# A GRU that runs one tile behind its attention instead of two, with VectorE's and ScalarE's work per tile dealt out to the chunks anew

## The chip, the cores and the metric

The kernel runs on one core of one Trainium2 chip. Its engines are TensorE (PE in the rows, PEld for its weight loads), VectorE (DVE), ScalarE (ACT), GpSimd (POOL) and SyncE (SP, which only issues DMAs here). Each engine works through its own list of instructions in order and meets the others only through semaphores. The metric is the device time of one execution in microseconds (us).

## The reference

For 4096 tokens of 256 features: a layer norm, a graph attention over a dense 0/1 adjacency matrix of 4096 x 4096, a GRU cell on the attention's result, a second layer norm, and a mixture of 16 experts of which each token uses two.

```
Wh = h @ W                                   # h = layernorm(x)
e = leaky_relu(Wh @ a1 + (Wh @ a2).T, 0.2)
att = softmax(where(adj > 0, e, -9e15))
h_prime = att @ Wh
gi = h_prime @ w_ih.T + b_ih ; gh = h @ w_hh.T + b_hh
r = sigmoid(i_r + h_r) ; z = sigmoid(i_z + h_z) ; n = tanh(i_n + r * h_n)
x = x + (1 - z) * n + z * h                  # called x1 below
x = x + experts(layernorm(x))                # top 2 of 16 by softmax(ln(x) @ gate_w + gate_b)
```

## The kernel before

There are three stages: a preparation of all 32 token tiles (up to about 115 us), the attention stage (about 115 to 843 us), which this change is about, and the routing tables with the 79 expert slots after it.

The attention stage handles one tile of 128 query tokens per round, against all 4096 keys. Keys are taken in chunks of 512, `CPT` = 8 chunks per tile; masks and exponentials are taken in quarters of 1024, `Q` = 4 per tile. Every engine has a hand-written function `body(i)` that is unrolled for i = 0, 1, ...; what an engine does in a round, and in which order, is the order of the lines in its `body`. `live(i, lag)` says whether tile i - lag exists. For tile i:

- ScalarE `logits(i, q)` (L546) and VectorE `less_one(i, q)` (L729, adjacency minus one), `mask_logits(i, q)` (L735), `row_max(i)` (L744, L745), then ScalarE `weights(i, q)` (L551, the exponential). This is made in round i - 1, one tile ahead. `row_max` needs all four masks and `weights` needs `row_max`.
- For each chunk TensorE transposes four 128 x 128 blocks into a PSUM bank (`transpose_weights`, L1012 on `E`), ScalarE copies the bank's high part (`chunk_hi`, L482 into `pc`), VectorE makes the low part (`chunk_lo`, L751), and TensorE adds 12 matmuls to the tile's sum (`accumulate`, L1106 to L1108). Transposes, `chunk_hi` and `chunk_lo` run two chunks ahead of `accumulate`, with three buffers each.
- When a tile's eight chunks are done, VectorE `combine` (L757, L760, divides the sum) and `remake_xn` (L767), TensorE `transpose_h` (L1012 on `scr` and `xnb`), ScalarE `copy_hT` (L482 into `hT`), TensorE `gru` (L1130, L1133, 16 matmuls), VectorE `gru_logits` (L772, L773), ScalarE `rz_tanh` (L573), VectorE `gru_n` (L778, L780), ScalarE `n_tanh` (L577), VectorE `gru_out` (L786 to L791, writes x1).
- Then the second norm: VectorE `norm2` (L796 to L798, then, when GpSimd's power L434 is done, L802 writes `xrow`), TensorE `transpose_x2` (L1012 on `xrow`), ScalarE `copy_x2T` (L482 into `xn2T`), TensorE `gate` (L1154), VectorE `route_top` (L809 to L816), ScalarE `gate_exp` (L587), VectorE `route_weights` (L822 to L824), after which SyncE stores the token's row.

Before, round i works on the sums of tile i, the GRU of tile i - 2 and the gate of tile i - 3, and there are T + 3 = 35 rounds, three of them behind the last sum. After the last round TensorE counts ranks (L1186), which waits for `route_weights` of the last tile and opens the routing stage.

Of the kernel before, what the change touches and what calls it, by code (L numbers as in the profile page):

```python
# [35 lines left out]
def gnn_moe(nc, x, adj, W, a, w_ih, w_hh, b_ih, b_hh, gate_w, gate_b, w1, w2, w3, out, rows):  # L36
# [24 lines left out]
    with ctx:  # L61
# [197 lines left out]

        block = ctx.enter_context(nc.Block())  # L260

        LAST = T + 3

        def live(i, lag):

# [48 lines left out]
        @block.sync  # L314
        def _(sp):
            row = lambda b, lo, hi: b[lo:hi].rearrange("(o f) -> o f", o=1).broadcast_to([P, hi - lo])
            xg4 = x.rearrange("(g r p) f -> g p r f", r=4, p=P)

            def load_x(g):
                k = g % 4  # L320
                if g >= 4:
                    sp.wait_ge(s_xn, (g - 3) * 4)
                sp.dma_start(xs[:, k * 4:k * 4 + 4, :], xg4[g]).then_inc(s_x[k], 16)

            load_x(0)
            sp.dma_start(Wn[:, :, :], W.rearrange("(k p) f -> p k f", p=P)).then_inc(s_cld[0], 16)
            sp.dma_start(a_row[:, :], a.rearrange("f o -> o f").broadcast_to([P, 2 * F])).then_inc(s_cld[1], 16)
            load_x(1)
            sp.dma_start(wnat[:, 0, :, :], w_ih.rearrange("(r p) f -> p r f", p=P)).then_inc(s_wn[0], 16)
            load_x(2)  # L330
            sp.dma_start(wnat[:, 1, :, :], w_hh.rearrange("(r p) f -> p r f", p=P)).then_inc(s_wn[1], 16)
            load_x(3)
            sp.dma_start(gwt[:, :, :], gate_w.rearrange("(k p) e -> p k e", p=P)).then_inc(s_cld[2], 16)
            sp.dma_start(gbias[:, :], row(gate_b, 0, NE)).then_inc(s_cld[3], 16)
            sp.dma_start(bias_rz[:, :], row(b_ih, 0, 2 * F)).then_inc(s_bld, 16)
            sp.dma_start(bhh_rz, row(b_hh, 0, 2 * F)).then_inc(s_bld, 16)
            sp.dma_start(bias_n[:, 0:F], row(b_ih, 2 * F, 3 * F)).then_inc(s_bld, 16)
            sp.dma_start(bias_n[:, F:2 * F], row(b_hh, 2 * F, 3 * F)).then_inc(s_bld, 16)
            for g in range(4, NG):
                load_x(g)  # L340

            def body(i):
                u = i % 2
                if live(i, 1):
                    v = (i - 1) % 2
                    if i >= 3:
                        sp.wait_ge(s_x1, i - 2)
                    sp.dma_start(xin[:, v, :], x[(i - 1) * P:i * P, :]).then_inc(s_xr[v], 16)
                if live(i, 2):
                    sp.wait_ge(s_x1, i - 1)  # L350
                    sp.dma_start(out[(i - 2) * P:(i - 1) * P, :], x1).then_inc(s_x1s, 16)
                if live(i, 3):
                    sp.wait_ge(s_row, i - 2)
                    sp.dma_start(rows[(i - 3) * P:(i - 2) * P, :], xrow[:, (i - 3) % 2, :]).then_inc(s_rows[(i - 3) % 2], 16)

            for i in range(LAST):
                body(i)


            w1v, w2v = (w.rearrange("e (p k) h -> e p (k h)", k=KB) for w in (w1, w2))  # L360
            w3v = w3.rearrange("e (p k) o -> e p (k o)", k=HB)
            sp.wait_ge(s_tab, 3)

            def load(s, r, m, st):

                if st == SLOTS:
                    return
                e, new, b = (table(sp, k, s) for k in (EXPERT, NEW, BUF))
                waits = []
                if st is None or st >= GR:  # L370
                    waits.append((s_whi, s * 2 + (1 - 2 * GR)))
                if st is None or st >= WB:
                    waits.append((s_fy, s - (WB - 1)))
                if waits:
                    wait_apart(sp, *waits)
                for n, wv in enumerate((w1v, w2v, w3v)):
                    sp.dma_start(wexp[:, one(b), n, :].rearrange("p o f -> p (o f)"),
                                 wv[one(e), :, :].rearrange("o p f -> (o p) f"), cond=new == 1).then_inc(s_w[r], 16)

            slot_iterations(sp, load)  # L380
            sp.wait_ge(s_sc, 16 * SLOTS)
# [3 lines left out]
        def _(pool):  # L385
# [39 lines left out]
                load_adj(1, q)  # L425

            def body(i):
                if i + 2 < T:
                    for q in range(Q):
                        pool.wait_ge(s_ms, (i + 1) * Q + q + 1)  # L430
                        load_adj(i + 2, q)
                if live(i, 2):
                    pool.wait_ge(s_var2, i - 1)
                    nc.gpsimd.tensor_tensor(rs[:, :], var[:, :], mhalf[:, :], ALU.pow).then_inc(s_rs2, 1)  # L434

            for i in range(LAST):
                body(i)
# [43 lines left out]
        def _(act):  # L481
# [103 lines left out]
            def gate_exp(i):  # L585
                act.wait_ge(s_dl, i - 2)
                nc.scalar.activation(rt[:, 1:2], rt[:, 0:1], ACT.Exp).then_inc(s_de, 1)  # L587

            def body(i):
                if live(i, 3):  # L590
                    act.wait_ge(s_t2, i - 2)
                    act_copy(xn2T[:, :, :].rearrange("p k m -> p (k m)"), tp[:, 0:F]).then_inc(s_t2e, 1)
                if i + 1 < T:
                    for q in range(Q):
                        logits(i + 1, q)
                for c in range(CPT):
                    if live(i, 0):
                        chunk_hi(i * CPT + c + 2)
                    if 1 <= c < 1 + Q and i + 1 < T:
                        weights(i + 1, c - 1)  # L600
                    if c == 2 and live(i, 2):
                        rz_tanh(i)
                    if c == 5 and live(i, 1):
                        copy_hT(i)
                    if c == 4 and live(i, 2):
                        n_tanh(i)
                    if c == 4 and live(i, 3):
                        gate_exp(i)

            for i in range(LAST):  # L610
                body(i)
# [54 lines left out]
        def _(dve):  # L666
# [123 lines left out]
                    dve.wait_ge(s_x1s, (i - 2) * 16)  # L790
                V_.tensor_tensor(x1, dd, xin[:, u, :], ALU.add).then_inc(s_x1, 1)  # L791

            def norm2(i):
                u = i % 2
                dve.wait_ge(s_x1, i - 1)
                link(V_.bn_stats(bst[:, 0, :], x1))  # L796
                link(V_.bn_aggr(mv[:, :], bst[:, 0, :]))
                V_.tensor_scalar(var[:, :], mv[:, 1:2], EPS, None, ALU.add).then_inc(s_var2, 1)  # L798
                dve.wait_ge(s_rs2, i - 1)
                if i >= 4:  # L800
                    dve.wait_ge(s_rows[u], ((i - 4) // 2) * 16 + 16)
                V_.tensor_scalar(xrow[:, u, 0:F], x1, mv[:, 0:1], rs[:, 0:1], ALU.subtract, ALU.mult).then_inc(s_ln2, 1)  # L802
# [39 lines left out]

            def body(i):
                ahead = i + 1 < T
                if ahead:
                    less_one(i + 1, 0)
                    less_one(i + 1, 1)
                if live(i, 1):
                    combine(i - 1)
                    remake_xn(i - 1)  # L850
                if ahead:
                    mask_logits(i + 1, 0)
                    less_one(i + 1, 2)
                    mask_logits(i + 1, 1)
                    less_one(i + 1, 3)
                    mask_logits(i + 1, 2)
                for c in range(CPT):
                    if live(i, 0):
                        chunk_lo(i * CPT + c + 2)
                    if c == 0 and ahead:  # L860
                        mask_logits(i + 1, 3)
                        row_max(i + 1)
                    if c == 1 and live(i, 2):
                        gru_logits(i)
                    if c == 2 and live(i, 3):
                        route_top(i)
                    if c == 3 and live(i, 2):
                        gru_n(i)
                    if c == 4 and live(i, 3):
                        route_weights(i)  # L870
                    if c == 5 and live(i, 2):
                        gru_out(i)
                    if c == 6 and live(i, 2):
                        norm2(i)

            for i in range(LAST):
                body(i)
# [132 lines left out]
        def _(pe):  # L1010
# [150 lines left out]
            transpose_weights(1)  # L1161

            def body(i):
                if live(i, 3):
                    transpose_x2(i)
                if live(i, 2):
                    gru(i)
                if live(i, 3) and not live(i, 0):
                    gate(i)
                for c in range(CPT):  # L1170
                    if live(i, 0):
                        transpose_weights(i * CPT + c + 2)
                        accumulate(i, c)
                    if c == 0 and live(i, 3) and live(i, 0):
                        gate(i)
                    if c == 3 and live(i, 1):
                        transpose_h(i)

            for i in range(LAST):
                body(i)  # L1180
# [90 lines left out]
```

## Time and profile before

| | |
|---|---|
| median of 3 runs | 1316.3 us (1313.3 to 1320.53) |
| the profiled execution | 1322.15 us, span 1320.4 us |
| busy share of the span: PE, PEld, DVE, ACT, POOL | 91%, 78%, 77%, 59%, 27% |
| TensorE clock, mean over the span | 0.945 of full speed |
| attention stage, 250 to 700 us: busy share PE, DVE, ACT | 98%, 85%, 67% |
| between 830 and 900 us: busy share PE, DVE | 43%, 82% |

The shares are of different stages: TensorE is busy nearly all the time in the attention rounds and in the expert slots, and waits at the end of the attention stage and through the routing tables. The profiled execution's own time beside its span leaves 1.75 us around it.

### The profile page before, as it was taken

The numbers are of one execution on the slowest core, as the hardware profiler recorded it, in microseconds if no ns is written. First come the engines' busy times: TensorE is split into PE (matmuls) and PEld (weight loads), VectorE is DVE, ScalarE is ACT, GpSimd is POOL, SyncE is SP. The second block draws the span as 40 slices with busy tenths as digits, with TensorE's granted clock in tenths as the row PEclk, the third lists the DMA queues.
The fourth block names the chain that finished last, engine by engine and source line by source line (L and its number), as shares of the span: only waits on it lengthen the run. The fifth ranks groups of instructions, "written<-read, shape, count | busy, mean of one in ns | idle before, by whom it ended". The sixth has DMA issues, their size and how long they took to land.

```text
span 1320.4 us, 25406 instructions
## 1 busy us (share of the span) xinstructions
PE 1195.2 (91%) x7317; PEld 1035.0 (78%) x7319; DVE 1019.8 (77%) x2445; ACT 779.5 (59%) x1141; POOL 355.0 (27%) x351
## 2 busy tenths in 40 slices
PE   5675999999999999999999997259999999999995
PEld 4445888888888898989898986148888888888884
DVE  5336788888888888888888875688888888888883
ACT  3227666666666666666666652006666666666662
POOL 1322111010101011111111100015656555555553
PEclk9767999999999999999999998659999999999998
DMA  6204424242424242424243400042354364345430
GB/s 200 56 1 64 63 55 77 57 77 57 77 57 77 57 77 56 77 57 77 57 77 57 77 25 21 13 150 53 52 137 96 55 187 135 91 93 146 93 48 8
DMA packets 61630, 98.60 MB, mean 75 GB/s; under 512 B 9472, under 2 KB 36096, under 8 KB 61536
## 3 DMA queue, kind: packets, MB, share of 16 engines
q0 software_dynamic: 33600, 52.49, 25.3%
q1 hardware_dynamic: 27936, 44.93, 10.5%
q8 instruction: 50, 0.82, 0.3%
q14 instruction: 44, 0.36, 0.1%
HBM read 213.18 MB, written 18.81 MB: 176 GB/s over the span
## 4 chain that ended last, share of the span: by engine, by line
PE 61%; DVE 16%; DMA 9%; ACT 6%; issue 4%; POOL 3%; POOLq 0%; DVEq 0%; SPq 0%; ACTq 0%
PE bank L1221 11%; PE bank L1012 11%; DMA out<-ysc,cidx 9%; PE bank L1130 8%; PE bank L1235 7%; PE bank L1107 5%; PE bank L1106 5%; PE bank L1108 5%; PE bank L1133 4%; DVE pc L751 3%; ACT E L551 2%; PE bank L1040 2%; ACT pc L482 1%; POOL rs L434 1%; DVE scr L788 1%
## 5 line engine op out<-in xcount | busy, mean ns | idle before, releaser
L1106 PE MATMUL bank<-V,pc 128*128 128x258 f32 x1024 | 311.2, 304 | 3.5 <-DVE pc L751 3.5
L1107 PE MATMUL bank<-V,pc 128*128 128x258 f32 x1024 | 291.6, 285 | 0.0
L1108 PE MATMUL bank<-V,pc 128*128 128x258 f32 x1024 | 289.3, 283 | 0.0
L482 ACT ACTIVATE pc<-bank 128x512 fp32r<-128x512 f32 x256 | 152.1, 595 | 173.0 <-PE bank L1012 169.6
L1221 PE MATMUL bank<-wup,xT 128*128 128x512 f32 x948 | 239.4, 401 | 0.9 <-DVE xT L959 0.9
L751 DVE TENSOR_TENSOR pc<-bank,pc 128x512 fp32r<-128x512 f32 x256 | 176.4, 689 | 64.4 <-ACT pc L482 59.9
L1221 PEld LDWEIGHTS bank<-wup,xT 128*128 128x128 f32 x948 | 174.4, 191 | 35.1 <-DVE xT L959 1.3
L1106 PEld LDWEIGHTS bank<-V,pc 128*128 128x128 f32 x1024 | 194.0, 189 | 4.6 <-DVE pc L751 4.6
L1108 PEld LDWEIGHTS bank<-V,pc 128*128 128x128 f32 x1024 | 196.1, 192 | 0.0
L1107 PEld LDWEIGHTS bank<-V,pc 128*128 128x128 f32 x1024 | 196.1, 191 | 0.0
L954 DVE TENSOR_TENSOR wup<-wexp,wup 128x1024 fp32r<-128x1024 f32 x158 | 185.8, 1217 | 2.3 <-ACT wup L482 1.4
L462 POOL DMA_INDIRECT out<-ysc,cidx x79 | 138.6, 1755 | 168.0 <-DMA out<-ysc,cidx 79.6
L482 ACT ACTIVATE wup<-wexp 128x1024 fp32r x158 | 165.6, 1050 | 9.2 <-DMA wexp<-in_L_ffn_w 8.6
L1012 PE MATMUL bank<-ident,E 128*128 128x128 f32 x1024 | 156.6, 276 | 13.4 <-ACT E L551 13.4
L735 DVE CUSTOM_DVE_ANT_0 E<-E,adjb 128x1024 f32<-128x1024 f32 x128 | 158.8, 1241 | 4.1 <-ACT E L546 3.8
L551 ACT ACTIVATE E<-E,nmu 128x1024 f32<-128x1024 f32 x128 | 146.3, 1145 | 11.8 <-DVE nmu L745 11.5
L1235 PE MATMUL bank<-wexp,hidT 128*128 x632 | 149.9, 380 | 1.3 <-ACT hidT L482 0.8
L387 POOL DMA_DIRECT2D adjb<-in_adj x128 | 69.5, 543 | 253.2 <-DVE dmx L735 249.5
L1012 PEld LDWEIGHTS bank<-ident,E 128*128 128x128 f32 x1024 | 122.9, 145 | 17.9 <-issue 14.9
L546 ACT ACTIVATE E<-Dp,sS 128x1024 f32<-128x1024 f32 x128 | 136.2, 1138 | 0.0
L1235 PEld LDWEIGHTS bank<-wexp,hidT 128*128 128x128 f32 x632 | 114.6, 191 | 14.0 <-issue 1.6
L434 POOL TENSOR_TENSOR rs<-var,mhalf 128x1 f32<-128x1 f32 x32 | 18.0, 561 | 391.1 <-DVE var L798 391.1
(155 smaller groups left out, 1645.4 us busy)
## 6 DMA issues: line engine op xcount, KB each, us to landing
wexp<-in_L_ffn_w SPq DMA_DIRECT2D x237, 512.0 KB
adjb<-in_adj POOLq DMA_DIRECT2D x128, 256.0 KB, 4.6
token_rows<-xrow SPq DMA_DIRECT2D x32, 130.0 KB, 2.2
E<-in_x SPq DMA_DIRECT2D x8, 512.0 KB, 5.3
xin<-in_x SPq DMA_DIRECT2D x32, 128.0 KB, 2.7
out<-xin SPq DMA_DIRECT2D x32, 128.0 KB, 1.7
xg<-token_rows,gidx POOLq DMA_INDIRECT x79, 3.6
out<-ysc,cidx POOLq DMA_INDIRECT x79, 3.8
```

The lines of the kernel that those rows point to most:

```text
L462: nc.gpsimd.indirect_dma_start(out=out[:, :], out_offset=bass.IndirectOffsetOnAxis(ap=cidx[:, s:s + 1], axis=0), in_=ysc[:, s % WR, :], in ...
L482: act_copy = lambda o, i: nc.scalar.activation(o, i, ACT.Copy)
L551: nc.scalar.activation(E[:, n % 2, cols], E[:, n % 2, cols], ACT.Exp, scale=1.0 / LSC, bias=nmu[:, n % 2, 0:1]).then_inc(s_ex, 1)
L735: V_.tensor_tensor_reduce(out=E[:, n % 2, cols], in0=E[:, n % 2, cols], in1=adjb[:, q, :], scale=1.0, scalar=-1e30, op0=ALU.add, op1=ALU.m ...
L751: V_.tensor_tensor(pc[:, C % 3, 1, :], pT[C % 3][:, :], pc[:, C % 3, 0, :].bitcast(F32), ALU.subtract).then_inc(s_plo, 1)
L954: V_.tensor_tensor(wup[:, r % 2, n, 1, :], wexp[:, one(b), n, :].rearrange("p o f -> p (o f)"), wup[:, r % 2, n, 0, :].bitcast(F32), ALU.s ...
L1012: tr = lambda o, i: nc.tensor.transpose(o, i, ident[:, :])
L1106: mm(acc[:, 0:VW], hi, V[:, j, 0, :], start=j == 0, stop=False)
L1107: mm(acc[:, 0:VW], hi, V[:, j, 1, :], start=False, stop=False)
L1108: ins = mm(acc[:, 0:VW], lo, V[:, j, 0, :], start=False, stop=j == T - 1)
L1221: ins = mm(acc[:, 0:HID], xT[:, r % WR, a, k * P:(k + 1) * P], wup[:, r % 2, n, b, k * HID:(k + 1) * HID], start=(k, a, b) == terms[0], st ...
L1235: ins = mm(accp[:, 0:F], hidT[:, k, :], wexp[:, one(b1), 2, k * F:(k + 1) * F].rearrange("p o f -> p (o f)"), start=k == 0, stop=k == HB - 1)
```

## The change

The number of rounds becomes T + 2. Round i now holds the sums of tile i, the GRU of tile i - 1 and the gate of tile i - 2. The second norm is split: `norm2_statistics` stands first in VectorE's round, its last part behind `combine` and `remake_xn`. The four masks and `less_one`, `logits` and `weights` are dealt to other chunks. The functions themselves, apart from that split, compute what they did.

```diff
-        LAST = T + 3
+        LAST = T + 2
 ScalarE, body(i):
-                if live(i, 3):
-                    act.wait_ge(s_t2, i - 2)
-                    act_copy(xn2T[:, :, :].rearrange("p k m -> p (k m)"), tp[:, 0:F]).then_inc(s_t2e, 1)
-                if i + 1 < T:
-                    for q in range(Q):
-                        logits(i + 1, q)
+                ahead = i + 1 < T
                 for c in range(CPT):
+                    if c < Q and ahead:
+                        logits(i + 1, c)
                     if live(i, 0):
                         chunk_hi(i * CPT + c + 2)
-                    if 1 <= c < 1 + Q and i + 1 < T:
-                        weights(i + 1, c - 1)
+                    if c == 1 and live(i, 1):
+                        copy_hT(i)
                     if c == 2 and live(i, 2):
-                        rz_tanh(i)
-                    if c == 5 and live(i, 1):
-                        copy_hT(i)
-                    if c == 4 and live(i, 2):
-                        n_tanh(i)
-                    if c == 4 and live(i, 3):
-                        gate_exp(i)
+                        copy_x2T(i + 1)
+                    if c == 3 and ahead:
+                        weights(i + 1, 0)
+                        weights(i + 1, 1)
+                    if c == 4 and live(i, 1):
+                        rz_tanh(i + 1)
+                    if c == 4 and ahead:
+                        weights(i + 1, 2)
+                        weights(i + 1, 3)
+                    if c == 5 and live(i, 2):
+                        gate_exp(i + 1)
+                    if c == 5 and live(i, 1):
+                        n_tanh(i + 1)
 VectorE, body(i):
-                if ahead:
-                    less_one(i + 1, 0)
-                    less_one(i + 1, 1)
+                if live(i, 2):
+                    norm2_statistics(i)
                 if live(i, 1):
                     combine(i - 1)
                     remake_xn(i - 1)
+                if live(i, 2):
+                    norm2(i)
                 if ahead:
-                    mask_logits(i + 1, 0)
-                    less_one(i + 1, 2)
-                    mask_logits(i + 1, 1)
-                    less_one(i + 1, 3)
-                    mask_logits(i + 1, 2)
+                    less_one(i + 1, 0)
                 for c in range(CPT):
                     if live(i, 0):
                         chunk_lo(i * CPT + c + 2)
-                    if c == 0 and ahead:
+                    if c < 3 and ahead:
+                        mask_logits(i + 1, c)
+                        less_one(i + 1, c + 1)
+                    if c == 2 and ahead:
                         mask_logits(i + 1, 3)
                         row_max(i + 1)
-                    if c == 1 and live(i, 2):
-                        gru_logits(i)
-                    if c == 2 and live(i, 3):
-                        route_top(i)
-                    if c == 3 and live(i, 2):
-                        gru_n(i)
-                    if c == 4 and live(i, 3):
-                        route_weights(i)
-                    if c == 5 and live(i, 2):
-                        gru_out(i)
+                    if c == 3 and live(i, 1):
+                        gru_logits(i + 1)
+                    if c == 4 and live(i, 2):
+                        route_top(i + 1)
+                    if c == 5 and live(i, 1):
+                        gru_n(i + 1)
                     if c == 6 and live(i, 2):
-                        norm2(i)
+                        route_weights(i + 1)
+                    if c == 7 and live(i, 1):
+                        gru_out(i + 1)
 TensorE, body(i):
-                if live(i, 3):
-                    transpose_x2(i)
-                if live(i, 2):
-                    gru(i)
-                if live(i, 3) and not live(i, 0):
-                    gate(i)
                 for c in range(CPT):
                     if live(i, 0):
                         transpose_weights(i * CPT + c + 2)
                         accumulate(i, c)
-                    if c == 0 and live(i, 3) and live(i, 0):
-                        gate(i)
-                    if c == 3 and live(i, 1):
+                    if c == 1 and live(i, 1):
                         transpose_h(i)
+                    if c == 2 and live(i, 2):
+                        transpose_x2(i + 1)
+                    if c == 2 and live(i, 1):
+                        gru(i + 1)
+                    if c == 2 and live(i, 2):
+                        gate(i + 1)
```

GpSimd's power moves ahead of its round's adjacency loads, and SyncE's loads of `xin` move one round later in its list. On TensorE the GRU now stands between the third and the fourth chunk of a round, where it stood ahead of the first.

ScalarE, from the start of a round before the change. `E<-Dp,sS` is `logits`, `E<-E,nmu` is `weights`, `pc` is `chunk_hi`, the 512-wide `scr` is `rz_tanh`, the 256-wide one `n_tanh`:

```order
L482 ACTIVATE xn2T<-bank4 128x256
L546 ACTIVATE E<-Dp,sS 128x1024 x4
L482 ACTIVATE pc<-bank6 128x512
L482 ACTIVATE pc<-bank7 128x512
L551 ACTIVATE E<-E,nmu 128x1024
L482 ACTIVATE pc<-bank5 128x512
L551 ACTIVATE E<-E,nmu 128x1024
L573 ACTIVATE scr<-scr 128x512
L482 ACTIVATE pc<-bank6 128x512
L551 ACTIVATE E<-E,nmu 128x1024
L482 ACTIVATE pc<-bank7 128x512
L551 ACTIVATE E<-E,nmu 128x1024
```

And from the third chunk of a round after the change (the same operations stand one line number lower; `rt` is `gate_exp`):

```order
L545 ACTIVATE E<-Dp,sS 128x1024
L481 ACTIVATE pc<-bank5 128x512
L481 ACTIVATE xn2T<-bank4 128x256
L545 ACTIVATE E<-Dp,sS 128x1024
L481 ACTIVATE pc<-bank6 128x512
L550 ACTIVATE E<-E,nmu 128x1024 x2
L481 ACTIVATE pc<-bank7 128x512
L572 ACTIVATE scr<-scr 128x512
L550 ACTIVATE E<-E,nmu 128x1024 x2
L481 ACTIVATE pc<-bank5 128x512
L586 ACTIVATE rt<-rt 128x1
L576 ACTIVATE scr<-scr 128x256
```

One exponential used to stand between two `chunk_hi`; now two stand between them, twice in a row, behind the `chunk_hi` of the chunk whose transposes TensorE issues after the GRU, and `n_tanh` stands in front of the last two `chunk_hi`.

VectorE, the end of one round and the start of the next, before (L751 is `chunk_lo`, L791 the last operation of `gru_out`, L729 `less_one`):

```order
L791 TENSOR_TENSOR xin<-scr,xin 128x256
L751 TENSOR_TENSOR pc<-bank,pc 128x512
L796 BN_STATS bst<-xin 128x6
L797 BN_AGGR mv<-bst 128x2
L798 TENSOR_SCALAR var<-mv 128x1
L802 TENSOR_SCALAR xrow<-xin,mv,rs 128x256
L751 TENSOR_TENSOR pc<-bank,pc 128x512
L729 TENSOR_SCALAR adjb<-adjb 128x1024 x2
L757 RECIPROCAL rden<-bank 128x1
L760 TENSOR_SCALAR scr<-bank,rden 128x256
L767 TENSOR_SCALAR xnb<-xin,xmv,rstd 128x256
L735 ISA E,dmx<-E,adjb 128x1024
```

The same place after; L757 is now `chunk_lo`, L797 the last of `gru_out`, L735 `less_one`, L763, L766 and L773 `combine` and `remake_xn`:

```order
L797 TENSOR_TENSOR xin<-scr,xin 128x256
L801 BN_STATS bst<-xin 128x6
L802 BN_AGGR mv<-bst 128x2
L803 TENSOR_SCALAR var<-mv 128x1
L763 RECIPROCAL rden<-bank 128x1
L766 TENSOR_SCALAR scr<-bank,rden 128x256
L773 TENSOR_SCALAR xnb<-xin,xmv,rstd 128x256
L810 TENSOR_SCALAR xrow<-xin,mv,rs 128x256
L735 TENSOR_SCALAR adjb<-adjb 128x1024
L757 TENSOR_TENSOR pc<-bank,pc 128x512
```

`gru_out` moved from two `chunk_lo` ahead of the round's end to behind the last one, and the statistics, `combine`, `remake_xn`, the end of the norm and one `less_one` now stand between it and the next `chunk_lo`.

## Rows read from the trace of the kernel before

**Rows 1.** Windows, 400 to 550 us: window, length, PE busy, granted clock, DMA
```profile
400.00:550.00 150.00, 147.18 (x1060) 1.00 0.38 67
```

**Rows 2.** Chain that ended last, in order of time: start, us, what
```profile
174.28 0.44 PE bank L1012 x2
...
786.75 0.44 PE bank L1012 x2
...
830.02 0.69 DVE scr L772
...
842.65 1.50 PE bank L1186 x3
```

**Rows 3.** Timeline of TensorE, one round: start, us, operation, idle before
```profile
349.32 0.44 PE L1012 MATMUL bank<-ident,xrow 128*128 128x128 f32 x2 [0.41 <-DVE xrow L802]
...
354.76 0.60 PE L1012 MATMUL bank<-ident,E 128*128 128x128 f32 x4
...
358.91 0.60 PE L1012 MATMUL bank<-ident,E 128*128 128x128 f32 x4
359.27 0.37 PE L1106 MATMUL bank<-V,pc 128*128 128x258 f32 x1
...
360.79 0.60 PE L1012 MATMUL bank<-ident,E 128*128 128x128 f32 x4
```

**Rows 4.** Timeline of ScalarE, the same round
```profile
359.55 0.60 ACT L482 ACTIVATE pc<-bank 128x512 fp32r<-128x512 f32 x1
360.04 1.15 ACT L551 ACTIVATE E<-E,nmu 128x1024 f32<-128x1024 f32 x1
361.08 0.62 ACT L573 ACTIVATE scr<-scr 128x512 f32<-128x512 f32 x1
361.60 0.59 ACT L482 ACTIVATE pc<-bank 128x512 fp32r<-128x512 f32 x1
...
365.29 0.41 ACT L577 ACTIVATE scr<-scr 128x256 f32<-128x256 f32 x1
```

**Rows 5.** Timeline of VectorE, the same round
```profile
349.78 0.75 DVE L729 TENSOR_SCALAR adjb<-adjb 128x1024 bf16<-128x1024 bf16 x2
350.45 0.16 DVE L757 RECIPROCAL rden<-bank 128x1 f32<-128x1 f32 x1
...
351.04 0.41 DVE L767 TENSOR_SCALAR xnb<-xin,xmv,rstd 128x256 f32<-128x256 f32 x1
351.36 1.22 DVE L735 CUSTOM_DVE_ANT_0 E<-E,adjb 128x1024 f32<-128x1024 f32 x1
...
362.22 0.69 DVE L751 TENSOR_TENSOR pc<-bank,pc 128x512 fp32r<-128x512 f32 x1
...
363.28 0.43 DVE L780 SCALAR_TENSOR_TENSOR scr<-scr 128x256 f32<-128x256 f32 x1
...
365.82 0.15 DVE L822 TENSOR_SCALAR rt<-rt 128x1 f32<-128x1 f32 x1 [0.74 <-ACT rt L587]
...
366.91 0.41 DVE L786 TENSOR_TENSOR scr<-xnb,scr 128x256 f32<-128x256 f32 x1
...
368.28 0.43 DVE L791 TENSOR_TENSOR xin<-scr,xin 128x256 f32<-128x256 f32 x1
...
369.23 0.42 DVE L796 BATCH_NORM_STATS2 bst<-xin 128x6 f32<-128x256 f32 x1
...
369.89 0.15 DVE L798 TENSOR_SCALAR var<-mv 128x1 f32<-128x1 f32 x1
370.73 0.41 DVE L802 TENSOR_SCALAR xrow<-xin,mv,rs 128x256 f32<-128x256 f32 x1 [0.68 <-POOL rs L434]
```

**Rows 6.** Timeline of TensorE in round 1, its first row and its wait
```profile
133.79 0.60 PE L1012 MATMUL bank<-ident,E 128*128 128x128 f32 x4
...
140.21 0.39 PE L1106 MATMUL bank<-V,pc 128*128 128x258 f32 x1 [2.08 <-DVE pc L751]
```

**Rows 7.** Windows: length, busy of PE, PEld, DVE, ACT, POOL, granted clock, DMA
```profile
139.50:145.50 6.00, 5.29 (x31) 5.29 (x32) 3.99 (x10) 3.79 (x5) 1.08 (x2) 0.72 0.90 145
```

More of the change, by code:

```diff
@@ L342, in body @@
             def body(i):
[L343 to L348, printed above, removed]
                 if live(i, 2):
@@ L351, in body @@
                     sp.dma_start(out[(i - 2) * P:(i - 1) * P, :], x1).then_inc(s_x1s, 16)
-                if live(i, 3):
-                    sp.wait_ge(s_row, i - 2)
-                    sp.dma_start(rows[(i - 3) * P:(i - 2) * P, :], xrow[:, (i - 3) % 2, :]).then_inc(s_rows[(i - 3) % 2], 16)
+                if live(i, 0):
+                    v = i % 2
+                    if i >= 2:
+                        sp.wait_ge(s_x1, i - 1)
+                    sp.dma_start(xin[:, v, :], x[i * P:(i + 1) * P, :]).then_inc(s_xr[v], 16)
+                if live(i, 2):
+                    sp.wait_ge(s_row, i - 1)
+                    sp.dma_start(rows[(i - 2) * P:(i - 1) * P, :], xrow[:, i % 2, :]).then_inc(s_rows[i % 2], 16)
             for i in range(LAST):
@@ L427, in body @@
             def body(i):
+                if live(i, 2):
+                    pool.wait_ge(s_var2, i - 1)
+                    nc.gpsimd.tensor_tensor(rs[:, :], var[:, :], mhalf[:, :], ALU.pow).then_inc(s_rs2, 1)
                 if i + 2 < T:
@@ L431, in body @@
                         load_adj(i + 2, q)
-                if live(i, 2):
-                    pool.wait_ge(s_var2, i - 1)
-                    nc.gpsimd.tensor_tensor(rs[:, :], var[:, :], mhalf[:, :], ALU.pow).then_inc(s_rs2, 1)
             for i in range(LAST):
@@ L587, in gate_exp, with copy_x2T @@
                 nc.scalar.activation(rt[:, 1:2], rt[:, 0:1], ACT.Exp).then_inc(s_de, 1)
+            def copy_x2T(i):
+                act.wait_ge(s_t2, i - 2)
+                act_copy(xn2T[:, :, :].rearrange("p k m -> p (k m)"), tp[:, 0:F]).then_inc(s_t2e, 1)
             def body(i):
-                if live(i, 3):
-                    act.wait_ge(s_t2, i - 2)
-                    act_copy(xn2T[:, :, :].rearrange("p k m -> p (k m)"), tp[:, 0:F]).then_inc(s_t2e, 1)
-                if i + 1 < T:
-                    for q in range(Q):
-                        logits(i + 1, q)
+                ahead = i + 1 < T
                 for c in range(CPT):
+                    if c < Q and ahead:
+                        logits(i + 1, c)
                     if live(i, 0):
                         chunk_hi(i * CPT + c + 2)
-                    if 1 <= c < 1 + Q and i + 1 < T:
-                        weights(i + 1, c - 1)
+                    if c == 1 and live(i, 1):
+                        copy_hT(i)
                     if c == 2 and live(i, 2):
-                        rz_tanh(i)
-                    if c == 5 and live(i, 1):
-                        copy_hT(i)
-                    if c == 4 and live(i, 2):
-                        n_tanh(i)
-                    if c == 4 and live(i, 3):
-                        gate_exp(i)
+                        copy_x2T(i + 1)
[9 more added lines that the diff above has]
+                        gate_exp(i + 1)
+                    if c == 5 and live(i, 1):
+                        n_tanh(i + 1)
             for i in range(LAST):
@@ L791, in gru_out, with norm2_statistics @@
                 V_.tensor_tensor(x1, dd, xin[:, u, :], ALU.add).then_inc(s_x1, 1)
-            def norm2(i):
-                u = i % 2
+            def norm2_statistics(i):
                 dve.wait_ge(s_x1, i - 1)
@@ L798, in norm2 @@
                 V_.tensor_scalar(var[:, :], mv[:, 1:2], EPS, None, ALU.add).then_inc(s_var2, 1)
+            def norm2(i):
+                u = i % 2
                 dve.wait_ge(s_rs2, i - 1)
@@ L844, in body @@
                 ahead = i + 1 < T
-                if ahead:
-                    less_one(i + 1, 0)
-                    less_one(i + 1, 1)
+                if live(i, 2):
+                    norm2_statistics(i)
                 if live(i, 1):
@@ L850, in body @@
                     remake_xn(i - 1)
+                if live(i, 2):
+                    norm2(i)
                 if ahead:
-                    mask_logits(i + 1, 0)
-                    less_one(i + 1, 2)
-                    mask_logits(i + 1, 1)
-                    less_one(i + 1, 3)
-                    mask_logits(i + 1, 2)
+                    less_one(i + 1, 0)
                 for c in range(CPT):
@@ L1163, in body @@
             def body(i):
-                if live(i, 3):
-                    transpose_x2(i)
-                if live(i, 2):
-                    gru(i)
-                if live(i, 3) and not live(i, 0):
-                    gate(i)
                 for c in range(CPT):
```

## The prediction

> **What bounds the kernel now.** I read the windows first. In the attention rounds TensorE is busy 147.18 of 150 us at the full clock, 2.4 GHz [rows 1], so little can be won there. The chain gives the length of a round: `transpose_x2` opens round 3 at 174.28 and round 31 at 786.75 [rows 2], 28 rounds, 612.47 us, **21.87 us each**. TensorE's timeline shows the only wait in a round: 0.41 us for `xrow` [rows 3]. The chain also prices the drain: from the start of round 31 to the rank matmuls at 842.65 it is 55.90 us [rows 2], in which the GRUs of the last two tiles run one after another with nothing beside them.
>
> What TensorE itself needs in a round: a chunk with its transposes 1.88 us (358.91 to 360.79), `transpose_x2` and the GRU 5.44 (349.32 to 354.76), the gate 0.39 (354.76 to 358.91 less two chunks) [rows 3], `transpose_h` 0.44, as the four transposes that it is. Eight chunks make 15.04, together **21.31 us**. A perfect order could win 0.56 us in each round.
>
> **What the change does.** It adds and removes no work in a round. It has two effects: one drain round less, and another ring of waits between the three engines. I walk that ring, as it now stands in the queues, from the transposes behind the GRU (chunk 5's, issued at c = 3; call their start 0).
>
> ScalarE: `chunk_hi` 5 can start 0.64 after the transposes did (358.91 to 359.55) [rows 3, 4] and holds the engine 0.49; one exponential holds it 1.04, `rz_tanh` 0.52 [rows 4]. The queue is hi 5, two exponentials, hi 6, `rz_tanh`, two exponentials, hi 7: 0.64 + 0.49 + 2.08 + 0.49 + 0.52 + 2.08 = 6.30. The exponentials need `row_max`, which VectorE finished during the GRU, so they don't wait.
>
> VectorE then takes over. `chunk_lo` 7 starts 0.62 after hi 7 (361.60 to 362.22) [rows 4, 5]: 6.92. `gru_n` stands behind it, and `n_tanh` can start 1.52 after that `chunk_lo` did (362.22 to 363.28, 0.43 of duration, 0.03 of signal) [rows 5]: 8.44. ScalarE's next `chunk_hi` (chunk 0 of the next tile) is queued behind `n_tanh`, which holds it 0.31 (0.41 less the 0.10 by which successors overlap) [rows 4]: 8.75; its `chunk_lo` starts at 9.37, holds VectorE 0.60, then `route_weights` and one more `chunk_lo` 1.09 (365.82 to 366.91) [rows 5]: `gru_out` starts at 11.06. To its last operation 1.37 (366.91 to 368.28), then 0.46, because the statistics now follow at once and must wait for x1 to be written: 12.89. Statistics 0.66 and about 0.08 for their last small operation, `combine` 0.59 (350.45 to 351.04), `remake_xn` 0.32, `xrow` the same shape, 0.32, `less_one` 0.33 (half of 349.78 to 350.45) [rows 5]: `chunk_lo` 2 starts at 15.19. GpSimd's power is back in time: 12.89 + 0.66 + 0.84 (369.89 to 370.73) [rows 5] = 14.39, against 14.54 when `xrow` is due, a margin of 0.15.
>
> TensorE closes the ring: matmuls can follow a `chunk_lo` start by 0.74, its 0.69 and a signal of 0.05: 15.93. Twelve matmuls 1.52 (359.27 to 360.79), 5.44 and 0.39 as above [rows 3]: the next transposes behind a GRU start at **23.28 us**.
>
> So the ring, 23.28, is longer than TensorE's own 21.31, and sets the round. On TensorE the 1.97 us appear in three places. Chunk 0 of the next tile is due at 5 x 1.88 + 0.36 = 9.76 and possible at 10.11: 0.35. `transpose_h` would be due at 13.51 and needs `remake_xn`, done with signal at 14.66: **1.15**. Chunk 2 then is due at 15.46 and possible at 15.93: 0.47. The old order filled VectorE's and ScalarE's time during the GRU with three masks and four logits; now both run dry there (VectorE has 10.3 us of work from the round's start until `row_max`, the GRU's successor transposes come some 3 us later) and do what they still owe in a row.
>
> **The sum**, against the chain of the profiled execution, 1322.15 us with 1.75 around its span, 0.4% above the median. I apply it to the median.
>
> - Rounds 3 to 30: 28 x 23.28 = 651.8 instead of 612.5: **+39.4**.
> - Rounds 1 and 2 take 40.49 us now (133.79 to 174.28) [rows 2, 6], without a GRU in round 1 and with a wait of 2.08. New: 8 x 1.88 + 0.44 + 5.17 = 20.65, and 23.28: **+3.4**. Round 0 I leave at nothing; its masks only move behind sums that are there anyway, and a microsecond either way is in the range.
> - Round 31 and the drain, 55.90 now. New: without `less_one` the GRU's successor transposes come 13.55 after the round's start (23.28 - 0.33 - 9.40). `chunk_lo` 7 follows at 2 x 1.88 + 0.64 + 0.62 = 5.02 from there, as no exponentials are left, `gru_out` at 6.98, statistics 8.81, `combine` 9.55, `transpose_h` 10.58. Then 0.64 and about 0.63 for `copy_hT`, 0.27 for `transpose_x2`, 5.3 for the GRU: `gru_logits` at 17.4. From the last `gru_logits` to the rank matmuls the same operations stand as now, 830.02 to 842.65 [rows 2], 12.63. Together 43.6: **-12.3**.
>
> 39.4 + 3.4 - 12.3 = +30.5, so 1316.3 + 30.5 = **1347 us**. Loads and stores are not in it: each adjacency quarter is asked for when its mask is done, nearly a round before its `less_one`; `xin` is asked for at the end of the round before the one that ends ahead of its use; the x1 store has a round. Nothing behind SyncE's or GpSimd's waits is due in the round.
>
> Here a page can be weighed. The row shows `remake_xn` lasting 0.41 while its successor starts 0.32 after it (351.04 to 351.36) [rows 5], and I count 0.32. The Trainium skill, VectorE: DVE Perf Modes, section "The DRAIN you can't avoid", says that a next operation does not start until the pipe is empty (and exempts successors that aren't held). By its rule without the exemption my steps would be short by some 0.09 each at seven places, an estimate of +0.6 per round, and the time would be about 1364. The rows are of this kernel and I go by them.
>
> **Rivals.**
>
> 1. *The clock falls too.* In round 1 TensorE waited 2.08 us [rows 6] and the clock then fell to its lower level, 1.2 GHz, for a while: mean 0.72 over 6 us [rows 7], 0.28 x 6 = 1.7 us lost. 29 waits of 0.4 us never did that. The new round has 1.15 and 0.47 us of waiting 0.9 us apart, with only transposes between. If that is enough, work just ahead of and inside the GRU slows, which lies on the ring: in a third of the rounds +17, 1364; in each +49, 1396. The Trainium skill, TensorE: Matmul & The Clock Gate, section "HAM oscillation — how this bites in real kernels", describes loops that fall in every round; by that rule it is the 1396. Chance 0.22, of which a third for every round.
> 2. *The ring is shorter than walked.* Some ten steps are handovers that I took from other neighbours. At 22.19 us a round the sum is zero (39.4 becomes 8.9), so 1.1 us of 23.28 would have to be wrong. Rounds of 22.0 to 22.6 give 1311 to 1328; about 1320. Chance 0.17, half of it within 0.5%.
> 3. *TensorE stays the bound*, the other side: VectorE's and ScalarE's free time (15% and 33%) absorbs the new order, and the `xrow` wait disappears. Rounds 21.31: 28 x -0.56 = -15.7; rounds 1 and 2 +1.5; drain without stalls -13.8: 1288. For it speak those shares; against it that every step of the ring is a queue position, not load. It decides from a ring below 21.3, that is 2 us less than the rows give. Chance 0.14. That the drain doesn't get shorter I give nothing: one round less stands in the program.
>
> **How the numbers follow.** The walk as it stands has 0.47, between 22.9 and 23.7 us a round, 1335 to 1360. The predicted time is that one. Range: upwards the clock in up to half of the rounds, 1375; downwards rival 2 to its lower end, 1310. Outside stay rival 3 (0.14) and the clock in most rounds (0.07). A measurement of this kernel tells about 0.5%, 6.6 us, from no change. Faster: 0.14 and a little of rival 2, 0.15; within 0.5%: 0.08; slower: 0.77.
>
> **What the profile after would show.** Right: rounds of about 23.3 us; TensorE at some 92% in the rounds; waits in each round for `xnb` (L773) ahead of `transpose_h` of about 1.1 us and for `chunk_lo` (L757) of some tenths, none for `xrow`; VectorE idle 2 to 3 us in front of the `chunk_lo` that follows `row_max`, ScalarE idle over 4 us in front of its `chunk_hi`; from the last round's start to the ranks about 44 us. Wrong: a round under 22.2 us; `transpose_h` not waiting; a clock below 1.00 between 400 and 550 us, which makes it rival 1; a wait for `in_adj` or `in_x` in the rounds, which I have priced at nothing.

## The result and the profile after

The changed kernel takes 1346.62 us (median of 4 runs, 1343.55 to 1354.01) against 1318.41 us before (4 runs): a ratio of 1.0213, 95% interval 1.0138 to 1.0287. The forecast was 1347. The profiled execution took 1347.14 us, its span is 1345.4.

The windows of the changed kernel (window, length, busy time of PE, PEld, DVE, ACT, POOL, granted clock, DMA), against [rows 1]:

```profile
400.00:550.00 150.00, 142.32 (x1014) 125.59 (x1013) 117.20 (x308) 93.51 (x138) 16.86 (x31) 1.00 0.37 63
```

TensorE does 142.32 us of work in 150, where it did 147.18, at the same clock. Who it waited for, from 150 to 790 us (us in total, times, longest):

```profile
PE bank L1018 <- DVE scr L766: 28.1, 28, 1.0
```

That is one wait of 1.0 us in each round, in front of `transpose_h`. The view names L766 (`combine`), the input of its first transposes; the semaphore that comes last is that of `remake_xn` (L773), as the timelines show. The wait for `xrow` of [rows 3] is gone. The chain of the changed kernel gives the length of a round by the starts of the GRU in rounds 3 and 30:

```profile
186.37 3.44 PE bank L1136 x8
...
813.93 3.44 PE bank L1136 x8
```

That is 627.56 us for 27 rounds, **23.24 us** each, where it was 21.87.

One round of TensorE in the changed kernel (L1018 on `E` opens a chunk's transposes):

```profile
400.92 0.63 PE L1018 MATMUL bank<-ident,E 128*128 128x128 f32 x4
...
410.35 0.60 PE L1018 MATMUL bank<-ident,E 128*128 128x128 f32 x4
...
412.60 0.60 PE L1018 MATMUL bank<-ident,E 128*128 128x128 f32 x4
...
415.66 0.41 PE L1018 MATMUL bank<-ident,scr 128*128 128x128 f32 x2 [1.03 <-DVE scr L766]
...
416.12 0.60 PE L1018 MATMUL bank<-ident,E 128*128 128x128 f32 x4
...
418.41 0.39 PE L1018 MATMUL bank<-ident,xrow 128*128 128x128 f32 x2
...
424.16 0.63 PE L1018 MATMUL bank<-ident,E 128*128 128x128 f32 x4
```

From one group of transposes behind a GRU to the next it is 23.24 us. The chunk that starts at 410.35 takes 2.25 us instead of 1.88, the one at 416.12 takes 2.29: these are two short waits, of 0.37 and 0.41 us. They don't show in the list of waits, where idle time begins at a matmul's modelled end; the distances of the chunks' starts show them. `transpose_h` starts 1.18 us after its place (412.60 + 1.88 = 414.48).

ScalarE, the same round:

```profile
401.59 0.60 ACT L481 ACTIVATE pc<-bank 128x512 fp32r<-128x512 f32 x1 [4.57 <-PE bank L1018]
402.08 2.18 ACT L550 ACTIVATE E<-E,nmu 128x1024 f32<-128x1024 f32 x2
...
405.16 2.18 ACT L550 ACTIVATE E<-E,nmu 128x1024 f32<-128x1024 f32 x2
407.24 0.59 ACT L481 ACTIVATE pc<-bank 128x512 fp32r<-128x512 f32 x1
...
409.38 0.42 ACT L576 ACTIVATE scr<-scr 128x256 f32<-128x256 f32 x1 [1.46 <-DVE scr L786]
409.70 1.07 ACT L481 ACTIVATE pc<-bank 128x512 fp32r<-128x512 f32 x2
```

And VectorE:

```profile
402.22 0.69 DVE L757 TENSOR_TENSOR pc<-bank,pc 128x512 fp32r<-128x512 f32 x1 [1.37 <-ACT pc L481]
...
407.86 0.69 DVE L757 TENSOR_TENSOR pc<-bank,pc 128x512 fp32r<-128x512 f32 x1 [1.13 <-ACT pc L481]
...
410.31 0.69 DVE L757 TENSOR_TENSOR pc<-bank,pc 128x512 fp32r<-128x512 f32 x1 [0.97 <-ACT pc L481]
...
411.97 0.42 DVE L792 TENSOR_TENSOR scr<-xnb,scr 128x256 f32<-128x256 f32 x1
...
413.81 0.43 DVE L801 BATCH_NORM_STATS2 bst<-xin 128x6 f32<-128x256 f32 x1
...
414.56 0.16 DVE L763 RECIPROCAL rden<-bank 128x1 f32<-128x1 f32 x1
...
415.15 0.41 DVE L773 TENSOR_SCALAR xnb<-xin,xmv,rstd 128x256 f32<-128x256 f32 x1
415.47 0.41 DVE L810 TENSOR_SCALAR xrow<-xin,mv,rs 128x256 f32<-128x256 f32 x1
...
416.13 0.68 DVE L757 TENSOR_TENSOR pc<-bank,pc 128x512 fp32r<-128x512 f32 x1
```

Counted in us from 400.92, as the walk of the prediction is counted from its start:

| step | forecast | measured |
|---|---|---|
| `chunk_hi` 7 starts | 6.30 | 6.32 |
| `n_tanh` | 8.44 | 8.46 |
| `chunk_lo` of the next tile's chunk 0 | 9.37 | 9.39 |
| `gru_out` | 11.06 | 11.05 |
| statistics | 12.89 | 12.89 |
| `combine` | 13.63 | 13.64 |
| `remake_xn` | 14.22 | 14.23 |
| `chunk_lo` 2 | 15.19 | 15.21 |
| transposes behind the next GRU | 23.28 | 23.24 |

The boundaries of the sum, TensorE's timeline of the changed kernel: the start of rounds 1, 3 and 31, and the rank matmuls.

```profile
134.49 0.60 PE L1018 MATMUL bank<-ident,E 128*128 128x128 f32 x4
...
177.93 0.60 PE L1018 MATMUL bank<-ident,E 128*128 128x128 f32 x4
...
828.73 0.60 PE L1018 MATMUL bank<-ident,E 128*128 128x128 f32 x4
...
873.20 1.03 PE L1190 MATMUL bank<-pick,before 128*128 128x512 bf16 x2 [1.89 <-DVE xrow L832]
```

| part | before | after | difference | forecast |
|---|---|---|---|---|
| up to round 1 | 133.79 | 134.49 | +0.7 | 0 |
| rounds 1 and 2 | 40.49 | 43.44 | +2.95 | +3.4 |
| rounds 3 to 30 | 612.47 | 650.80 | +38.3 | +39.4 |
| round 31 and drain | 55.90 | 44.47 | -11.4 | -12.3 |
| behind the rank matmuls | 477.75 | 472.2 | -5.5 | 0 |

### The profile page after: what moved, and what is told of

It reads as the page before. It is cut to its first block, busy times and chain, and to the rows that moved or that the text cites. A ratio compares the mean times of both kernels' runs of the same rounds, so it can differ in the third digit from the quotient of the medians.

```text
span 1345.4 us, 25407 instructions
## 1 busy us (share of the span) xinstructions
PE 1206.3 (90%) x7318; PEld 1035.8 (77%) x7319; DVE 1015.6 (75%) x2445; ACT 767.1 (57%) x1141; POOL 355.6 (26%) x351
## 4 chain that ended last, share of the span: by engine, by line
PE 54%; DVE 20%; ACT 16%; issue 6%; DMA 2%; POOL 1%; DVEq 0%; POOLq 0%; SPq 0%; ACTq 0%
PE bank L1225 16%; ACT E L550 10%; PE bank L1239 10%; PE bank L1136 8%; PE bank L1018 7%; ACT pc L481 5%; DVE pc L757 4%; PE bank L1139 4%; PE bank L1112 2%; PE bank L1046 2%; PE bank L1113 1%; PE bank L1114 1%; DVE bst L801 1%; DVE xin L797 1%; DVE scr L793 1%
## 5 line engine op out<-in xcount | busy, mean ns | idle before, releaser
L757 DVE TENSOR_TENSOR pc<-bank,pc 128x512 fp32r<-128x512 f32 x256 | 175.5, 687 | 144.3 <-ACT pc L481 144.3
L481 ACT ACTIVATE pc<-bank 128x512 fp32r<-128x512 f32 x256 | 148.0, 591 | 149.9 <-PE bank L1018 149.9
L461 POOL DMA_INDIRECT out<-ysc,cidx x79 | 134.8, 1707 | 161.3 <-DMA out<-ysc,cidx 81.4
L1018 PE MATMUL bank<-ident,E 128*128 128x128 f32 x1024 | 156.1, 276 | 13.4 <-ACT E L550 13.4
L545 ACT ACTIVATE E<-Dp,sS 128x1024 f32<-128x1024 f32 x128 | 146.4, 1146 | 0.0
L550 ACT ACTIVATE E<-E,nmu 128x1024 f32<-128x1024 f32 x128 | 139.6, 1143 | 7.1 <-DVE nmu L751 7.1
L1018 PEld LDWEIGHTS bank<-ident,E 128*128 128x128 f32 x1024 | 121.4, 144 | 15.0 <-issue 14.9
```

The lines of the kernel that those rows point to most:

```text
L481: act_copy = lambda o, i: nc.scalar.activation(o, i, ACT.Copy)
L545: nc.scalar.activation(E[:, n % 2, cols], Dp[:, cols], ACT.Relu, bias=sS[:, n:n + 1]).then_inc(s_pre, 1)
L550: nc.scalar.activation(E[:, n % 2, cols], E[:, n % 2, cols], ACT.Exp, scale=1.0 / LSC, bias=nmu[:, n % 2, 0:1]).then_inc(s_ex, 1)
L757: V_.tensor_tensor(pc[:, C % 3, 1, :], pT[C % 3][:, :], pc[:, C % 3, 0, :].bitcast(F32), ALU.subtract).then_inc(s_plo, 1)
L1018: tr = lambda o, i: nc.tensor.transpose(o, i, ident[:, :])
```

## The experiments

The theory is that a ring of waits over all three engines (VectorE waits for ScalarE, TensorE for VectorE, and ScalarE for TensorE again) is longer than TensorE's work and sets the round. There are three other readings: the wait for `transpose_h` is a matter of its place in TensorE's list; VectorE's load sets the round; a single queue position is the fault. The length of a round below is always the mean distance of GRU starts in TensorE's timeline over 22 rounds in the middle; ratios are to the kernel before on the same chip.

**a_ntanh.** One line of ScalarE's round:

```diff
-                    if c == 5 and live(i, 1):
+                    if c == 6 and live(i, 1):
                         n_tanh(i + 1)
```

> The changed kernel with one line of ScalarE's round moved: n_tanh behind the next chunk_hi instead of ahead of it. My theory (the ring over ScalarE, VectorE and TensorE sets the round): chunk_hi of the next tile's chunk 0 no longer waits for gru_n, its chunk_lo starts behind gru_n at 8.3 instead of 9.4 us after the transposes behind the GRU, gru_out starts at 10.0 instead of 11.1, and the round falls by 1.05 us from 23.24 to about 22.2; about -30 us. Rival 'TensorE's list puts transpose_h too early, the rest is hidden': ScalarE's order does not matter, 23.2 us a round, no change.

Measured: 22.19 us a round; 1319.35 us, ratio 0.9994 (0.9972 to 1.0017). ScalarE's order alone takes off 1.05 us a round and the whole loss: this version is as fast as the kernel before.

**b_split.** One exponential per chunk:

```diff
                     if c == 3 and ahead:
                         weights(i + 1, 0)
-                        weights(i + 1, 1)
                     if c == 4 and live(i, 1):
                         rz_tanh(i + 1)
                     if c == 4 and ahead:
-                        weights(i + 1, 2)
-                        weights(i + 1, 3)
+                        weights(i + 1, 1)
                     if c == 5 and live(i, 2):
                         gate_exp(i + 1)
+                    if c == 5 and ahead:
+                        weights(i + 1, 2)
                     if c == 5 and live(i, 1):
                         n_tanh(i + 1)
+                    if c == 6 and ahead:
+                        weights(i + 1, 3)
```

> The changed kernel with the four exponentials one per chunk (c = 3, 4, 5, 6) instead of two and two; n_tanh stays ahead of the next chunk_hi. My theory: chunk_hi 7 starts at about 4.6 instead of 6.3 us after the transposes behind the GRU, n_tanh at 6.7, gru_out at about 9.8 (then bound by TensorE's chunks through chunk_lo of the last chunk), so the round is about 22.0 us; about -35 us. Rival 'transpose_h too early': 23.2, no change.

Measured: 22.00 us a round; 1312.79 us, ratio 0.9937 (0.9914 to 0.9961). The same ScalarE work in another order is worth 1.24 us a round.

**c_shift.** `transpose_h`, `copy_hT`, `transpose_x2`, `copy_x2T`, `gru` and `gate` at c + 1 in TensorE's and ScalarE's rounds (two of the six moved lines are shown):

```diff
-                    if c == 1 and live(i, 1):
+                    if c == 2 and live(i, 1):
                         transpose_h(i)
...
-                    if c == 2 and live(i, 1):
+                    if c == 3 and live(i, 1):
                         gru(i + 1)
```

> The changed kernel with transpose_h, its copy, transpose_x2, its copy, the GRU and the gate one chunk later in TensorE's and ScalarE's rounds; VectorE's round as it is. My theory: transpose_h no longer waits, but the ring is as long as before, because chunk_lo 2 still stands behind gru_out, the statistics, combine and the rest: the wait moves to the matmuls of chunk 2, about 1.8 us, and the round is about 23.0 us; within 0.5% of the changed kernel. Rival 'transpose_h stands too early in TensorE's list': its 1.15 us vanish, 22.1 us a round, about -32 us.

Measured: 23.00 us a round; 1345.15 us, ratio 1.0183 (1.0149 to 1.0218). TensorE's waits in it, 200 to 780 us:

```profile
PE bank L1112 <- DVE pc L757: 37.4, 25, 1.5
```

The wait for `transpose_h` is gone from the list and one of 1.5 us for `chunk_lo` stands there instead (1.75 by the distance of the chunks' starts, against the 1.8 expected). The place of `transpose_h` was not the fault.

**d_both.** b_split, and `gru_out` one chunk earlier:

```diff
-                    if c == 7 and live(i, 1):
+                    if c == 6 and live(i, 1):
                         gru_out(i + 1)
```

> The changed kernel with the exponentials one per chunk and gru_out one chunk earlier in VectorE's round, ahead of the last chunk_lo, which also takes away its 0.12 us wait for x1. My theory: gru_out starts at about 8.7 us after the transposes behind the GRU, transpose_h no longer waits, 0.1 us is left at chunk 2: about 21.4 us a round, TensorE's own time; about 1295 us, faster than the kernel before and than the changed one. Rival: another limit (adjacency loads, clock) keeps the round above 22 us.

Measured: 21.40 us a round; 1288.91 us, ratio 0.9757 (0.9724 to 0.979), 6 us under the time expected. By its windows TensorE has no free time left:

```profile
400.00:550.00 150.00, 150.00 (x1082) 134.20 (x1081) 129.10 (x337) 101.93 (x148) 19.02 (x35) 1.00 0.40 69
```

The starts on TensorE still show a short wait. In one of its rounds chunk 2 begins at the first row and takes 2.05 us up to `transpose_x2`, where 1.88 is its length:

```profile
412.06 0.60 PE L1020 MATMUL bank<-ident,E 128*128 128x128 f32 x4
...
414.11 0.39 PE L1020 MATMUL bank<-ident,xrow 128*128 128x128 f32 x2
```

**f_gruout.** The changed kernel with this last diff alone.

> The changed kernel with gru_out alone one chunk earlier in VectorE's round (the exponentials stay two and two). My theory: since n_tanh is late, gru_out can start at 10.5 instead of 11.1 us after the transposes behind the GRU, but the last chunk_lo now waits behind it, its matmuls stand about 0.9 us, and the ring is hardly shorter: about 23.15 us a round instead of 23.24. Rival 'gru_out behind the last chunk_lo is the fault by itself': the 1.09 us of chunk_lo and route_weights ahead of it come off, 22.2.

Measured: 23.12 us a round, 1344.26 us (one run). Alone this edit is worth 0.12 us a round; on top of b_split it was worth 0.60 (22.00 to 21.40). Its position was a fault only once the exponentials were out of the way.

**e_less.** d_both, and the first `less_one` behind `chunk_lo` 2:

```diff
-                if ahead:
-                    less_one(i + 1, 0)
                 for c in range(CPT):
                     if live(i, 0):
                         chunk_lo(i * CPT + c + 2)
+                    if c == 0 and ahead:
+                        less_one(i + 1, 0)
```

> The kernel of the run d_both (exponentials one per chunk, gru_out one chunk earlier) with the first less_one of a round behind chunk_lo 2 instead of ahead of it. d_both has rounds of 21.41 us. My theory: its last wait, about 0.1 us at the matmuls of chunk 2, is what is left of the ring, and 0.33 us less ahead of that chunk_lo removes it: 21.31 us a round, TensorE's own time, about -3 us, which a timing can hardly tell but the rows can. Rival: TensorE needs 21.4 by itself, no change of the round.

Measured: 21.25 us a round; 1288.24 us, ratio 0.9768 (0.9738 to 0.9798). The round is 0.15 us shorter than in d_both: the short wait shown there is gone (chunk 2 takes 1.89 us here). TensorE's own time in a round is therefore at most 21.25, where the prediction had 21.31. The times of the two kernels can't be told apart.

**g_filler** and **h_filler_idle.** Four needless VectorE operations, once on the ring, once where VectorE waits:

```diff
                     combine(i - 1)
+                    if i >= 2:
+                        for k in range(4):
+                            V_.tensor_tensor(xnb[:, 4 + k, :], xnb[:, 2, :], xnb[:, 3, :], ALU.subtract)
                     remake_xn(i - 1)
```

In h_filler_idle the same loop stands behind `row_max(i + 1)` instead.

> The changed kernel with four needless VectorE operations of 128x256 (0.34 us each, on buffers that nobody reads) between combine and remake_xn, from round 2 on. My theory: they lie on the ring, each us costs a us: round 24.6 us, about +39 us for the kernel, and transpose_h waits 2.4 us. It also asks for the clock: if a wait of that length in each round brings the clock down, rounds get longer than 24.6 and the granted clock in the rounds falls below 1.00. Rival 'VectorE has a quarter of its time free': under 0.3 us a round.

> The changed kernel with the same four needless VectorE operations behind row_max, where VectorE waits 1.37 us for the chunk behind the GRU. My theory: not on the ring, round 23.24 to 23.3 us, no change. Rival 'VectorE's load per round sets the round': +1.4 us a round, as in g_filler.

Measured, h_filler_idle: 23.25 us a round, 1349.52 us (one run): the four operations cost nothing. g_filler: 1403.16 us (one run), rounds of 24.58 us at the least and up to 25.96, mean 25.16. The same 1.34 us cost nothing in one place and 1.34 us in the other, so the load of VectorE doesn't set the round. What lies above 24.58 is the clock. A round of g_filler in which it fell, TensorE's row behind the wait, and windows of 1.5 us around it:

```profile
434.95 0.41 PE L1021 MATMUL bank<-ident,scr 128*128 128x128 f32 x2 [2.37 <-issue]
```

```profile
433.00:434.50 1.50, 0.00 (x0) 0.00 (x0) 1.50 (x6) 0.00 (x0) 0.23 (x1) 1.00 0.33 98
434.50:436.00 1.50, 1.05 (x8) 0.86 (x8) 1.50 (x5) 0.38 (x1) 0.00 (x0) 1.00 0.00 0
436.00:437.50 1.50, 1.35 (x7) 1.34 (x7) 1.50 (x4) 1.50 (x3) 0.00 (x0) 0.58 0.00 0
437.50:439.00 1.50, 1.50 (x9) 1.50 (x8) 1.50 (x3) 0.24 (x1) 0.57 (x1) 0.50 0.26 25
439.00:440.50 1.50, 1.50 (x6) 0.98 (x5) 1.50 (x5) 0.97 (x2) 0.53 (x1) 0.78 0.82 122
```

The clock falls to its lower level (1.2 GHz) at about 436.2 and is back at about 439.7. The round before, with the same wait of 2.37 us, kept it. TensorE's windows around this fall and the next (window, length, PE busy, granted clock, DMA) show that it is not a matter of most rounds:

```profile
365.00:436.00 71.00, 63.27 (x447) 1.00 0.35 60
436.00:440.00 4.00, 3.85 (x17) 0.57 0.29 33
440.00:487.00 47.00, 41.74 (x295) 1.00 0.34 60
487.00:491.00 4.00, 4.00 (x16) 0.57 0.33 42
491.00:562.00 71.00, 63.25 (x447) 1.00 0.34 60
```

Over the middle of the stage the falls are 51 or 75 us apart, three in eight rounds. Most rounds are longer than 24.58 us because one fall lengthens two neighbouring ones, by 1.56 to 1.59 us together (25.96 and 24.76, 25.55 and 25.20, 25.74 and 24.98).

**i_filler2** and **i_filler3.** g_filler with two and three operations:

```diff
-                        for k in range(4):
+                        for k in range(2):
```

(and `range(3)` in the second).

> As g_filler, with two needless operations between combine and remake_xn instead of four. By the ring: 23.24 + 0.67 = 23.9 us a round and a wait of 1.7 us ahead of transpose_h. Open is the clock: at 1.0 us of wait it never fell, at 2.4 us in most rounds. If it already falls here, rounds scatter above 23.9; if not, all are 23.9.

> As g_filler, with three needless operations. By the ring: 24.25 us a round, wait 2.05 us. If the clock falls in some rounds they scatter above that; fewer of them than with four.

Measured: i_filler2 1376.74 us (one run), 23.91 us a round with one of 25.26 among them; i_filler3 1397.64 us (one run), 24.25 in most rounds, and about every fifth of 25.2 to 25.4 with a next one of 24.6 to 24.9, again 1.55 us together. "At 2.4 us in most rounds", from which i_filler2 started, was a misreading of round lengths: the granted clock has three falls in eight rounds there.

## Why the prediction was right

**What bounds the kernel.** Right: TensorE before, the ring after. h_filler_idle and g_filler show it from VectorE's side, a_ntanh and b_split from ScalarE's, c_shift from TensorE's.

**The ring, 23.28 us.** Measured were 23.24 us, and no step in the table of the walk is off by more than 0.04. The durations held because none of the operations had changed; what had to be right was the order of the queues, and which of several inputs comes last at each step. The same walk, now with the changed kernel's trace at hand, gave 22.2, 22.0, 23.0 and 21.4 for four other orders; measured were 22.19, 22.00, 23.00 and 21.40.

**The sum, +30.5.** The four parts in the attention stage came to +30.6. That it is so near is in part luck, since the parts were off by up to 1.1 us in both directions:

- Up to round 1 it took 0.7 more, in a round that I had left at nothing.
- Rounds 1 and 2 took 0.5 less. Round 1 has no `route_weights` ahead of `gru_out` yet, so the ring is shorter by that once, and `transpose_h` of round 2 waits 0.57 us instead of 1.03:

```profile
159.97 0.41 PE L1018 MATMUL bank<-ident,scr 128*128 128x128 f32 x2 [0.57 <-DVE scr L766]
```

- Rounds 3 to 30 took 1.1 less, 0.04 in each.
- The drain took 0.9 more, out of two larger errors. TensorE waits 2.0 us for `transpose_h` of the last tile, the clock falls, and that tile's GRU takes 4.82 us in its 512-wide part instead of the 3.44 of the tile before, which I had counted at the full clock. From that `transpose_h` to `gru_logits` it is 8.6 us, forecast were 6.8. From there to the rank matmuls it is 11.7 us (861.52 to 873.20), where I had kept the old 12.63; from the end of `gru_n` to `gru_out` alone it is 0.48 instead of 1.11, as `route_weights` now runs beside `n_tanh`.

The two 512-wide parts, in the chain of the changed kernel:

```profile
836.83 3.44 PE bank L1136 x8
...
854.93 4.82 PE bank L1136 x8
```

**The experts' stage** was counted as unchanged and was 5.5 us shorter in this pair of executions. It is 476.8 us in d_both's profile (813.34 to the end of the span, 1290.1) and 472.1 in e_less's, whose programs are the same there. In the twelve profiles of this case it is 471.4 to 472.2 us four times and 476.7 to 479.1 eight times, so it varies by this much from one execution to the next; why, no run here shows. The distance of the profiled executions, 25.0 us, is too small by that; the medians' is 28.2. The forecast time of 1347 was met within 0.4 us, and that is luck: the kernel before came out at 1318.41 instead of the 1316.3 that I started from, and the distance at 28.2 instead of 30.5.

**Waits.** Forecast were 0.35, 1.15 and 0.47, measured 0.37, 1.18 and 0.41; no wait for `in_adj` or `in_x` shows (a tile's load of `xin` stands one round earlier in SyncE's list than before, not later). Two signs were mis-sized. TensorE's busy share in the rounds is 95%, not some 92: the modelled ends hide part of its waits, by the starts it is 21.25 of 23.24 us, 91%. And VectorE's wait behind `row_max` is 1.37 us, not 2 to 3. I had set it from the nominal start of the round, and the ring's own delays push `row_max` later. Neither carried anything.

**The page on VectorE.** Behind `remake_xn`, 0.41 us long, the next operation came 0.32 later in the changed kernel too (415.15 to 415.47). Where an operation waits for the result of the one before, the step is longer: 0.45 to 0.46 inside `gru_out`, as the walk had it with 1.37 for three of them. By the rule of the Trainium skill, VectorE: DVE Perf Modes, section "The DRAIN you can't avoid", read without its exemption, the prediction's estimate was 1364; the measurement decides for the rows.

**The rivals.** The clock did not fall in the rounds (1.00 from 150 to 790 us). The rival was real all the same: with 0.7 us more of waiting it fell once (i_filler2), with 1.0 more in every fifth round (i_filler3). By the Trainium skill, TensorE: Matmul & The Clock Gate, section "HAM oscillation — how this bites in real kernels", a loop can fall in every round; its example waits some 3 to 5 us for a DMA each time, and the prediction's 1396 took over its outcome without such waits. Here no run fell in every round: it was three in eight at 2.4 us and none at 1.0. A ring shorter than walked fell with the table above; a_ntanh shows that its arithmetic was right, since with rounds of 22.19 us, where the prediction has the sum at zero, the ratio is 0.9994. TensorE as the bound, 1288 us, is what d_both reached: the change's idea, one tile less of lag, is worth what that rival said once the queues are in order.

## What to carry to other kernels

Where an engine is busy 98% of the time, a new order of the others can only be judged by the longest ring of waits through all queues: write down, from the rows of the old profile, when each step's last input is there, once around, and compare it with the busiest engine's own time. Free time on an engine is worth something only at the place where it lies; the same four operations cost nothing or their full length. Faults in an order hide one another: `gru_out`'s place was worth 0.12 us alone and 0.60 with the exponentials apart, so a single edit that brings nothing is no proof against it.

## What was not expected of the hardware

The clock's answer to a wait that recurs in each round is a matter of how often, not of yes or no. With TensorE waiting about 1.0 us in front of two pairs of transposes the clock stayed at 2.4 GHz in all rounds, and so it did with 1.5 us in front of chunk 2's matmuls (c_shift). With 1.7 us it fell in one round of 29, with 2.0 us in about every fifth, with 2.4 us in three of eight, to 1.2 GHz each time and for 3.4 us in the round shown. A fall cost 1.35 to 1.6 us, mostly shared by two neighbouring rounds. Rounds with the same wait and the same work went both ways, so one round that keeps the clock does not show that the next one will. It isn't chance either: in i_filler3 the falls came back every fifth round, in g_filler after two or three. What picks the round, no run here separates.
